# Factors for queries and output gate made ahead on GpSimd, and the first gated product moved between two taps of a convolution

## The reference

```python
mem = scan(a=gamma, b=i_gate * k * v)               # a linear recurrence along the tokens
out = _ln(mem, mn_g, mn_b) * q                       # heads of 16: centre, normalise, weight, shift
o = (out - mean) / sqrt(var + 1e-5)                  # per head again
o = o.reshape(.., C) * gn_g + gn_b
o = o * sigmoid(xc @ og_w.T + og_b)                  # the output gate
x = x + o @ Wo.T + hidden @ w3.T                     # hidden = sigmoid(xn @ w1) * (xn @ w2)
```

## Time and profile before

| what | value |
|---|---|
| runs of the kernel before | 848.96, 849.62, 851.63 us (median 849.62) |
| the profiled execution | 849.49 us |
| its span, first to last instruction | 847.5 us |
| busy in the span: PE, DVE, ACT, POOL | 88%, 75%, 55%, 50% |
| mean granted clock of PE | 0.949 of full speed |
| turns A, B, C and the last, from scan to scan | start at 658.7, 711.1, 760.9 and 813.6 us |

### The profile page before, as it was taken

The page is one execution under the profiler, slowest core; times in us unless marked ns, Lnnn a source line. Parts: engine busy times, 40 slices in busy tenths (PEclk is TensorE's granted clock), DMA queues, the critical chain, the costliest instruction groups (busy, mean ns, idle before and its releaser), DMA issues. The chain is left out here.

```text
span 847.5 us, 15157 instructions
## 1 busy us (share of the span) xinstructions
PE 742.0 (88%) x5602; PEld 638.1 (75%) x5602; DVE 633.5 (75%) x1099; ACT 468.4 (55%) x746; POOL 423.2 (50%) x369
## 2 busy tenths in 40 slices
PE   3368799999999999999999999999779797988773
PEld 2256678888888888888888888888567686877662
DVE  6999877788777686777778777674373998988966
ACT  4246645755655664665566565567656454664411
POOL 2344454354355667658535435436436373763831
PEclk9579999999999999999999999999889999999985
DMA  5111121111011010110100000021100000000000
GB/s 157 28 39 39 39 77 46 45 40 45 3 33 40 21 52 21 39 46 20 28 21 3 21 3 20 21 77 40 52 1 0 1 1 26 1 26 1 1 26 25
DMA packets 22108, 25.89 MB, mean 31 GB/s; under 512 B 4498, under 2 KB 17170, under 8 KB 22036
## 3 DMA queue, kind: packets, MB, share of 16 engines
q1 hardware_dynamic: 22036, 24.93, 10.4%
HBM read 14.83 MB, written 3.28 MB: 21 GB/s over the span
## 5 line engine op out<-in xcount | busy, mean ns | idle before, releaser
L652 DVE TENSOR_REDUCE neg_max<-s_pair 128x4 f32<-128x1024 f32 x127 | 155.0, 1221 | 75.5 <-PE s_pair L866 75.3
L474 ACT ACTIVATE probs<-t_pair 128x1024 f32<-128x1024 f32 x128 | 131.3, 1025 | 135.9 <-PE t_pair L891 135.6
L371 POOL TENSOR_TENSOR hid<-g,hid 128x512 f32<-128x512 f32 x64 | 82.1, 1283 | 177.7 <-DVE g L763 144.6
L365 POOL TENSOR_TENSOR hid_lo<-hid,hid_hi 128x512 fp32r<-128x512 f32 x64 | 85.5, 1336 | 82.7 <-ACT hid_hi L497 82.6
L866 PE MATMUL s_pair<-K,Q 96*128 96x256 f32 x508 | 84.8, 290 | 16.1 <-DVE neg_max L652 9.8
L866 PEld LDWEIGHTS s_pair<-K,Q 96*128 96x128 f32 x508 | 75.5, 194 | 24.5 <-issue 8.1
L891 PE MATMUL t_pair<-Q,K 104*128 104x512 f32 x256 | 85.6, 416 | 0.3 <-DMA Q<-max_parts 0.3
L933 PE MATMUL down<-hi,hid_hi 128*128 128x256 f32 x256 | 83.9, 328 | 0.8 <-POOL hid_lo L365 0.8
L906 PE MATMUL misc<-probs,V 128*32 128x256 f32 x1024 | 69.4, 389 | 4.0 <-DVE kc L608 2.5
L933 PE MATMUL down<-lo,hid_hi 128*128 128x256 f32 x256 | 71.5, 279 | 0.0
L933 PE MATMUL down<-hi,hid_lo 128*128 128x256 f32 x256 | 71.2, 278 | 0.0
(11 more groups left out here) (258 smaller groups left out, 1962.9 us busy)
## 6 DMA issues: line engine op xcount, KB each, us to landing
stage<-in_ternary SPq DMA_DIRECT2D x18, 256.0 KB, 2.8
Q<-q_hi SPq DMA_DIRECT2D x64, 64.0 KB, 2.0
stage<-in_scales SPq DMA_DIRECT2D x8, 384.0 KB, 3.3
X<-in_x SPq DMA_DIRECT2D x8, 256.0 KB, 4.4
Q<-q_lo SPq DMA_DIRECT2D x32, 64.0 KB, 2.0
Q<-max_parts SPq DMA_DIRECT2D x128, 4.0 KB
out<-X SPq DMA_DIRECT2D x8, 256.0 KB, 2.3
signs<-w_stage SPq DMA_DIRECT2D x9, 128.0 KB, 1.8
```

Of the source, the lines that this page charges most:

```text
L365: pool.tensor_tensor(hid_lo[:, m % 2, :, :].rearrange("p a n -> p (a n)"), hid[:, m % 2, :], hid_hi[:, m % 2, :, :].rearrange("p a n -> p ...
L371: pool.tensor_tensor(hid[:, m % 2, :], g[:, m % 2, :], hid[:, m % 2, :], ALU.mult).then_inc(S["hid_done"], 1)
L474: act.activation(probs[:, u % 2, th, :], t_pair[:], ACT.Exp, scale=SCALE).then_inc(S["probs_done"], 1)
L652: dve.tensor_reduce(neg_max[:, u % 2, 4 * jp:4 * jp + 4], score_banks(u, jp)[:].rearrange("p (s n) -> p s n", n=SEQ), AX_X, ALU.max, negat ...
```

## The change

- `queries_weighted`, new on POOL at the head of a turn, four instructions: `o = q_kept * mn_b` and `q_kept = q_kept * mn_g`, for both halves.
- `gates_weighted`, new on POOL right behind it, four instructions: once DVE has multiplied by `q_kept` (`mw_done`), `q_kept = gate * gn_b2` and `gate = gate * gn_g2`.
- `output_weighted(b)`, new on POOL, one instruction each between the steps of the early group: the centred output times the gate.
- `memory_scaled` and `gated` (six instructions on DVE and six on POOL in a turn) are gone. DVE gets instead a multiplication by `q_kept` behind each sum of `memory_summed`, an addition of `o` for each half in `memory_normed`, and an addition of `q_kept` for each half in `output_applied`.
- `hidden(0)` stands between taps 2 and 3.
- ACT's `queries_kept` stands behind `output_high`, since `q_kept` is in use until the additions of `output_applied`.
- In the last turn `mlp_added` stands behind `output_applied`. `ffn_down` waits for the additions of its half.

```diff
+                def queries_weighted():
+                    wait = waiter(pool, late)
+                    wait("q_kept", 1)
+                    wait("o_turned", 0)
...
+                    for b in range(BPG):
+                        inc(pool.tensor_tensor(heads(o[:, pair(b), :]), heads(q_kept[:, pair(b), :]), mn_b, ALU.mult), "mq_done")
+                    for b in range(BPG):
+                        wait("mq_done", b + 1)
+                        inc(pool.tensor_tensor(heads(q_kept[:, pair(b), :]), heads(q_kept[:, pair(b), :]), mn_g, ALU.mult), "mq_done")
+
+                def gates_weighted():
+                    wait = waiter(pool, late)
+                    wait("mw_done", BPG)
+                    wait("gates_done", TPG)
+                    for b in range(BPG):
+                        inc(pool.tensor_tensor(q_kept[:, pair(b), :], gates[:, 1 + late % 2, pair(b), :], gn_b2, ALU.mult), "gw_done")
+                    for b in range(BPG):
+                        g = gates[:, 1 + late % 2, pair(b), :]
+                        wait("gw_done", b + 1)
+                        inc(pool.tensor_tensor(g, g, gn_g2, ALU.mult), "gw_done")
+
+                def output_weighted(b):
+                    wait = waiter(pool, late)
+                    wait("cen_sq", b + 1)
+                    wait("gw_done", BPG + b + 1)
+                    inc(pool.tensor_tensor(o[:, pair(b), :], o[:, pair(b), :], gates[:, 1 + late % 2, pair(b), :], ALU.mult), "xg_done")
...
-                memory_scaled(pool, late, 1)
+                queries_weighted()
+                gates_weighted()
                 if early is not None:
                     hidden_low(pool, early, 1)
                     convolved()
                     hidden_low(pool, early, 2)
                     values(pool, early, 0)
+                output_weighted(0)
+                if early is not None:
                     hidden_low(pool, early, 3)
+                output_weighted(1)
+                if early is not None:
                     hidden_low(pool, early, 4)
                     through_input_gate(pool, early, 0)
-                gated(pool, late, 0)
...
                 if early is not None:
-                    queries_kept()
                     hidden_high(5)
                 for b in halves:
                     output_high(b)
+                if early is not None:
+                    queries_kept()
...
                         inc(dve.tensor_reduce(sm[:, b, :], osq[:, b, :].rearrange("p (h d) -> p h d", d=L1_DH), AX_X, ALU.add), "sm_done")
+                        wait("mq_done", BPG + b + 1)
+                        y = turned(banks[4 + b][:])
+                        inc(dve.tensor_tensor(y, y, q_kept[:, pair(b), :], ALU.mult), "mw_done")
...
-                    wait("o_turned", 0)
+                    wait("mw_done", BPG)
                     for b in range(BPG):
                         y = turned(banks[4 + b][:])
-                        inc(dve.tensor_tensor(heads(o[:, pair(b), :] if b else y), heads(y), each(sm[:, b, :]), ALU.mult), "mn_done")
+                        inc(dve.tensor_tensor(heads(y), heads(y), each(sm[:, b, :]), ALU.mult), "mn_done")
+                    for b in range(BPG):
+                        wait("mn_done", b + 1)
+                        inc(dve.tensor_tensor(o[:, pair(b), :], turned(banks[4 + b][:]), o[:, pair(b), :], ALU.add), f"op_done{b}")
...
-                    for b in range(BPG):
-                        y = turned(banks[5][:]) if b else o[:, pair(b), :]
+                    for b in halves:
+                        y = turned(banks[4 + b][:])
+                        wait("xg_done", b + 1)
                         inc(dve.tensor_tensor(heads(y), heads(o[:, pair(b), :]), each(s2[:, b, :]), ALU.mult), "on_done")
+                    for n, b in enumerate(halves):
+                        wait("on_done", n + 1)
+                        inc(dve.tensor_tensor(o[:, pair(b), :], turned(banks[4 + b][:]), q_kept[:, pair(b), :], ALU.add), f"o_done{b}")
...
                 if early is not None:
-                    convolve(early, range(2, TAPS))
+                    convolve(early, range(2, 3))
+                    hidden(0)
+                    convolve(early, range(3, TAPS))
                 memory_summed()
-                if early is not None:
-                    hidden(0)
                 memory_normed()
                 if early is not None:
                     hidden(1)
-                memory_scaled(dve, late, 0)
...
                 output_applied()
-                gated(dve, late, 1)
                 if early is not None:
                     hidden(5)
+                else:
+                    mlp_added(0)
+                    mlp_added(1)
...
-                        if b == 0:
-                            wait("op_done0", 1)
-                        wait("mn_done", b + 1)
+                        wait(f"op_done{b}", 1)
```

More of the change, by code:

```diff
@@ L1038, in layer1 @@
                    b_turned=BPG, scan_done=BPG, mem_centered=BPG, mem_sq=BPG, sm_done=BPG, rm_done=1, mn_done=BPG,
-                   op_link0=2, op_link1=2, op_done0=1, op_done1=1, so_done=BPG, cen_done=BPG, cen_sq=BPG, s2_done=BPG,
-                   ro_done=1, on_done=BPG, o_link0=2, o_link1=2, o_done0=1, o_done1=1,
+                   mq_done=4, mw_done=BPG, op_done0=1, op_done1=1, so_done=BPG, cen_done=BPG, cen_sq=BPG, s2_done=BPG,
+                   ro_done=1, on_done=BPG, gw_done=4, xg_done=BPG, o_done0=1, o_done1=1,
                    o_turned=BPG, o_hi_done=BPG, o_lo_done=BPG, y_done=BPG, res_done=BPG,
@@ L1157, in through_input_gate @@
             inc(engine.tensor_tensor(vn[:, pair(b), :], qk[:, 1, pair(b), :], gates[:, 0, pair(b), :], ALU.mult), f"b_done{b}")
-        def memory_scaled(engine, late, b):
-            wait = waiter(engine, late)
-            wait("mn_done", b + 1)
[L1162 to L1171, removed]
-            y = turned(banks[5][:]) if b else o[:, pair(b), :]
[L1173 to L1176, removed]
         @block.sync
@@ L1230, in convolved @@
                         inc(pool.tensor_tensor(xc_lo[:, k, :], cs[:, k, :], xc_hi[:, k, :].bitcast(F32), ALU.subtract), "xc_lo_done")
+                def queries_weighted():
+                    wait = waiter(pool, late)
+                    wait("q_kept", 1)
+                    wait("o_turned", 0)
+                    if late == 0:
+                        pool.wait_ge(once["scaled"], 4)
+                    for b in range(BPG):
[18 more added lines that the diff above has]
+                    inc(pool.tensor_tensor(o[:, pair(b), :], o[:, pair(b), :], gates[:, 1 + late % 2, pair(b), :], ALU.mult), "xg_done")
                 if late is None:
@@ L1366, in queries_kept @@
                     wait("norm_done", 1)
-                    wait("op_done0", 0)
-                    wait("op_done1", 0)
+                    wait("o_done0", 0)
+                    wait("o_done1", 0)
                     wait("ro_done", 0)
@@ L1610, in output_normed @@
                     wait("q_kept", 1)
-                    wait("mlp_done", 1)
+                    if early is not None:
+                        wait("mlp_done", BPG)
                     squared, root = (banks[4][:, n * BPG * PAIR_HEADS:(n + 1) * BPG * PAIR_HEADS] for n in range(2))
@@ L1684, in turn @@
                 output_summed()
-                if early is None:
-                    mlp_added(0)
-                    mlp_added(1)
                 output_normed()
```

## The result

The changed kernel takes 869.33 us (median of four runs, 867.8 to 869.91) against 849.29 for the kernel before in the same comparison: a ratio of 1.0231, 95% interval 1.0212 to 1.025. The forecast was 868 in a range from 853 to 874. The profiled execution took 869.0 with a span of 867.2, 19.7 more than before.

A forecast was written before the change was run, and what follows sets the result against it. DVE's list was taken to set a turn's middle, POOL and ACT its tail; turns A +6.8, B +7.5, C +2.7 and the last +1.6 gave +18.6 on 849.49, so 868 us, range 853 to 874.

The forecast's parts named there:

- The chain against the gate products: Memory's root: four POOL products of `gates_weighted` hold up DVE's nine short instructions, 4.5 us a turn, bounds 1.2 and 5.1.
- The rival of one wait only: Memory's root: DVE keeps the port once it has it, so a collision costs 1.2, not 4.5; 855 us, chance 0.12.
- that of a chain not held up: Memory's root: short DVE instructions slip in between POOL's reads and the clock holds; about 846 us, chance 0.10.
- The alternation of the earlier trace: Layer 0, profile before: DVE and POOL took turns on SBUF, each waiting out a whole instruction of the other.
- The start of `ffn_up(2)`: Middle of a turn: `ffn_up(2)` waits for the later `hidden(1)`, +5.3 us in turn A, +4.7 in B, +3.1 in C.
- PE's clock: Behind some 7 us of PE idle ahead of `ffn_up(2)` the clock falls: 1.5 us in each of three turns.
- the third rival: After the idle, `query_key(3)` and `output` also run at the lower clock, 2 us more a turn; about 874, chance 0.08.
- The tail: End of a turn, `output_weighted` collisions, earlier transposes, later tap 1 and residuals: 0 in A, +1.3 in B, -1.9 in C.
- What the edit gains, PE gives back ahead of `ffn_up(2)`: Early `hidden(0)` starts `ffn_up(1)` at about 715.5 instead of 718.00, but `hidden(1)` comes later, so nothing is gained.
- That `hidden(0)` brings nothing by itself is no rival: `hidden(0)` between the taps: its bringing no gain by itself was counted as part of the forecast.

The follow-up runs named there:

- The first edit alone: The changed kernel with `hidden(0)` put back behind the two sums and products, nothing else undone: 858.69 us, ratio 1.0119 to the kernel before.
- the second alone: The kernel before with `hidden(0)` moved between taps 2 and 3 and nothing else: 844.85 us, ratio 0.9947.
- all three edits: The changed kernel with `gates_weighted` behind the root, `hidden(1)` ahead of `memory_normed` and `first_tap` ahead of `queries_kept`: 845.64 us, ratio 0.9947 to the kernel before.

## Why the prediction was right, and where it was off

**The chain against the gate products: right.** I took 4.5 for it, from 1.2 to 5.1; it is 4.03 in turn B, and the runs with none, two and four of the products ahead of the root give 2.26, 4.37 and 6.3 us. The rival of one wait only needed one long line and falls, and so does that of a chain not held up: four lines are long in every turn. The alternation of the earlier trace rows holds for instructions of 64 elements as well. With several POOL products waiting, the two engines take strict turns. The Trainium skill, page "SBUF — State Buffer", section "Who interferes with whom", calls the port that the two engines share an exclusive lock, which whoever issues first holds for the whole instruction. The trace agrees: each long line lasts about as long as a POOL product (1.18 to 1.29 against 1.25 to 1.27).

**The start of `ffn_up(2)`: right in the whole, off in its parts.** Counted from the taps it comes later by 4.3, 5.3 and 3.8 us in turns A, B and C; the sum had 5.3, 4.7 and 3.1. A is less because the queries' products hold up the taps by 1.4 (2.40 + 1.82 against 1.39 + 1.41), not 2.1, and the chain by 4.0, not 4.5. B and C are more for a term that I did not have: `ffn_up(0)` runs slowly there, and `hidden(0)` waits 0.92 and 0.94 for it.

**PE's clock: right, one place missed.** `ffn_up(2)` takes 3.78 instead of 2.00 in each full turn, 1.8 where the sum had 1.5, at a granted 0.50 of full speed, that is 1.2 GHz. The place missed is `ffn_up(0)` in B and C. `query_key(3)`, slow in the third rival, does run slowly for the most part: `ffn_up(3)` starts 2.15 to 2.26 us after its start, where it was 1.57 before. That costs little, 0.25 to 0.37 of DVE's waiting for its squares (684.76 in turn A), and the projection of the output runs at full clock in A and B.

**The tail: right in kind.** Transposes come directly behind the projections in A and B, tap 1 is late by 1.10 us, and `output_weighted` holds up the second chain by about 0.9 (0.74 of it at L1639, which takes 0.96 instead of 0.22), where I took 1.4. What is left of each turn without `ffn_up(2)`'s delay and the clock's 1.8 is 5.84 - 4.3 - 1.8 = -0.3 in A, 8.12 - 5.3 - 1.8 = 1.0 in B and 3.90 - 3.8 - 1.8 = -1.7 in C; the forecast had 0, 1.3 and -1.9.

**Two readings of the trace before** were loose. In turn B DVE does not run to the end of its list with no idle of note: it waits 2.45 us for ACT ahead of `output_low` (756.01). The sum works the tail out by itself and does not rest on that. And the earlier trace rows set 64 elements beside 192; the fair measure of 192 is the 0.35 us of lines L1503 and L1504 just ahead, so the collision there is about 1.15 us and the reading stands.

**By turns**, forecast and measured: A 6.8 and 5.84, B 7.5 and 8.12, C 2.7 and 3.90, the last 1.6 and 1.62; together 18.6 and 19.5. The sum is close partly because A's overestimate pays for the slow `ffn_up(0)` of B and C.

**The step that failed** is "What the edit gains, PE gives back ahead of `ffn_up(2)`", with "That `hidden(0)` brings nothing by itself is no rival". With PE's clock full before and after, it is so (0.41 in turn B). But the edit changes how PE's idle is cut up, and so the clock: alone it gains 6.2 us of layer 1's time, and together with the held-up chain it costs 8.6, by gathering PE's idle in front of the chunk that DVE waits for next. The first edit alone costs 10.9 and the second alone gains 6.2; both together cost 19.5, not 4.6 (by the medians a cost of 8.2, a gain of 5.6 and a cost of 20.0). That the clock is what ties the two is read from the traces and was not tested by itself. The forecast got the sum of both right since it was worked out for both together, turn by turn, and would have been wrong for either alone.

## What to carry to other kernels

A POOL product that is released just as DVE begins a chain of short instructions on SBUF tiles cost DVE here about 1 us of its 1.26; look for such a meeting, and release the product behind the chain by one wait, where DVE does something that no engine is waiting for. When an edit removes a wait of PE, look at the length of the idle that is left and at what stands behind it: cutting one wait of 3 us into shorter ones can keep the clock, gathering them into one can lose it. Two edits that are each judged alone need not add when both move the same idle.

## What the runs showed of the hardware that was not expected

A `tensor_scalar` of 64 elements, one SBUF input and one SBUF output, is held up in full as well (L1513: 1.29 us against 0.20), not only instructions with two SBUF inputs.

The length of PE's idle does not alone say whether its clock falls. After 2.26 us in the changed kernel `ffn_up(0)` of turn B took 3.31; after 2.30 at the same place with `hidden(0)` back it took 2.09; after 2.41 ahead of `ffn_up(1)` of the kernel before nothing fell, and with all three edits 2.45 was followed by 3.58. With the gate products behind the root, `ffn_up(2)` of turn C took 2.11 after 2.64; with `hidden(0)` back as well, `ffn_up(1)` of turn C took 2.09 after 2.90, the longest of these. What decides between them was not settled by these runs.
